# One order of stages for another in the six lists that four engines play, in a two-layer transformer stack

## The reference

```python
x = x + ln(conv(ln(x)))      # filter phazor**t * init, over the 256 positions, through an FFT; y.real
x = x + ln(moe(ln(x)))       # 8 experts (128->64->128), top 2 of a softmax, silu(gate)*up, and a shared expert
x = x + ln(attention(ln(x))) # 16 heads of 64, q and k scaled to unit length, 2 null keys and values,
                             # alibi slopes, causal mask, softmax
x = x + ln(ffn(x))           # top 2 of 4 different experts:
#   e0 = silu(x@w1) * (x@w3) @ w2
#   e1 = gelu(linear chain(x)) @ c2        e3 = gelu(x@ml_w1 + b) @ ml_w2
#   e2: syn = x@w; h = ln(syn + attn(syn)); h = ln(h + relu(h@f1)@f2); h@gen
```

## Time and profile before

| | us |
|---|---|
| median of 3 runs | 1089.22 (1089.21 to 1092.03) |
| profiled execution | 1091.11 |
| its span | 1089.3 |
| PE busy | 967.2 (89%) |
| DVE busy | 815.8 (75%) |
| POOL busy | 585.1 (54%) |
| ACT busy | 568.5 (52%) |
| mean granted clock of TensorE | 0.972 of full speed |

### The profile page before, as it was taken

How to read it: one execution, slowest core, us unless ns; L and a number is a source line. 1 busy time by engine, 2 the same in 40 slices (tenths; PEclk the granted TensorE clock), 3 DMA queues, 4 the chain that set the end, 5 groups by cost and what they waited for, 6 DMA issues and landing times.

```text
span 1089.3 us, 22228 instructions
## 1 busy us (share of the span) xinstructions
PE 967.2 (89%) x8405; PEld 741.4 (68%) x8405; DVE 815.8 (75%) x2425; ACT 568.5 (52%) x1288; POOL 585.1 (54%) x570
## 2 busy tenths in 40 slices
PE   0777899899989999899989999899999999898987
PEld 0566767677766867667777777668776777667755
DVE  5788667978779687887778787886778665793556
ACT  4417642764437552774537643575527653385522
POOL 4227453854557463764737645674627644573623
PEclk9978999999999999999999999999999999899999
DMA  5300000000000000000000000000000000000000
GB/s 154 84 0 10 2 2 2 1 11 2 12 1 1 11 2 11 1 10 2 2 11 1 12 2 11 1 11 2 2 11 1 1 2 2 10 1 2 12 1 11
DMA packets 22091, 11.53 MB, mean 11 GB/s; under 512 B 7648, under 2 KB 21344, under 8 KB 21856
## 3 DMA queue, kind: packets, MB, share of 16 engines
q1 hardware_dynamic: 18272, 8.86, 3.1%
q10 hardware_dynamic: 3712, 1.25, 0.5%
HBM read 8.00 MB, written 2.10 MB: 9 GB/s over the span
## 4 chain that ended last, share of the span: by engine, by line
PE 39%; DVE 34%; POOL 14%; issue 6%; ACT 5%; ACTq 0%; DVEq 0%; POOLq 0%
POOL rnorm L869 9%; PE bank L1909 5%; PE bank L1907 3%; PE bank L1649 3%; PE bank L1870 3%; PE bank L1651 2%; PE bank L1650 2%; PE bank L2042 2%; DVE unit L1483 2%; PE bank L1656 2%; PE bank L2048 2%; DVE sumsq L1474 2%; PE bank L1800 2%; PE bank L1876 2%; DVE x4m L1601 1%
## 5 line engine op out<-in xcount | busy, mean ns | idle before, releaser
L869 POOL TENSOR_TENSOR rnorm<-sumsq,minus_half 128x16 f32<-128x16 f32 x64 | 185.7, 2932 | 11.1 <-DVE sumsq L1477 11.1
L877 POOL TENSOR_TENSOR square<-square,causal 128x256 f32<-128x256 f32 x128 | 97.7, 794 | 87.1 <-ACT square L1111 87.1
L877 POOL TENSOR_TENSOR unit<-unit,causal 128x256 f32<-128x256 f32 x128 | 89.9, 732 | 91.4 <-ACT unit L1111 91.3
L1870 PE MATMUL bank<-qT,kT 64*128 64x256 f32 x512 | 96.6, 389 | 0.0
L1106 ACT ACTIVATE square<-bank,bias_k 128x256 f32<-128x256 f32 x128 | 54.2, 483 | 69.7 <-PE bank L1870 69.6
L1483 DVE TENSOR_TENSOR unit<-unit,rnorm 128x1024 f32<-128x1024 f32 x64 | 79.1, 1240 | 10.5 <-POOL rnorm L869 9.6
L1474 DVE TENSOR_REDUCE sumsq<-square 128x16 f32<-128x1024 f32 x64 | 77.8, 1216 | 9.3 <-ACT square L1066 9.3
L1876 PE MATMUL bank<-qT,kT 64*128 64x128 f32 x512 | 84.1, 284 | 0.7 <-ACT val L1083 0.7
L1059 ACT ACTIVATE unit<-bank 128x512 f32<-128x512 f32 x128 | 72.3, 600 | 23.7 <-PE bank L1651 20.8
L1876 PEld LDWEIGHTS bank<-qT,kT 64*128 64x128 f32 x512 | 71.0, 186 | 16.8 <-issue 10.1
L1045 ACT ACTIVATE xaT_hi<-bank 128x256 fp32r<-128x256 f32 x16 | 6.0, 384 | 144.0 <-PE bank L1808 144.0
(11 more groups left out here) (385 smaller groups left out, 2772.8 us busy)
## 6 DMA issues: line engine op xcount, KB each, us to landing
xin<-in_L_attn_x SPq DMA_DIRECT2D x7, 256.0 KB, 2.8
out<-x SPq DMA_DIRECT2D x7, 256.0 KB, 2.3
square<-in_L_attn_w_kv SPq DMA_DIRECT2D x1, 1024.0 KB, 7.6
w_sw<-in_L_ffn_sw_w SPq DMA_DIRECT2D x3, 256.0 KB, 6.2
unit<-in_L_attn_w_q SPq DMA_DIRECT2D x1, 512.0 KB, 6.7
w_out<-in_L_attn_w_out SPq DMA_DIRECT2D x8, 64.0 KB, 2.1
w_ml<-in_L_ffn_ml_w SPq DMA_DIRECT2D x2, 256.0 KB, 5.7
xin<-in_L_attn_x ACTq DMA_DIRECT2D x1, 256.0 KB, 3.2
```

Of the source, the lines that this page charges most:

```text
L869: pool.tensor_tensor(rnorm[:, k, t, :], sumsq[:, t % 2, k, :], minus_half[:], ALU.pow).then_inc(a_root.sem, 1)
L877: m = pool.tensor_tensor(pd, pd, causal[:].unsqueeze(1).to_broadcast([P, 2, P]), ALU.mult)
L1870: return mm(bank[s][:, 2 * P * i:2 * P * (i + 1)], kT[rs, p, 2 * P * b:2 * P * b + P], qT[rs, p, 2 * P * b:2 * P * (b + 1)], start=True, s ...
```

## The change

All 24 lists (six tables, four engines) hold the same stages as before in another order. No function, no wait and no buffer is changed; all lines behind the tables stand two further down (L1808 before is L1810 after). The first lines of PE's list of the round:

```diff
 MIDDLE = {
     "PE": """
-a_m.0 a_m.1 f_clock f_turn.0 f_turn.1 f_ce.0 f_ce.1 f_sw.0 a_null f_me.0 a_t.0 f_sw.1 f_ceT a_m.2 f_relu.0 a_v.0 f_sw.2
+f_clock a_m.0 a_null f_turn.0 f_turn.1 f_ce.0 f_ce.1 a_m.1 f_sw.0 f_me.0 a_t.0 f_sw.1 f_ceT a_m.2 f_relu.0 f_relu.1
...
-a_out.1 l_x.1
+l_down.3 a_out.0 a_out.1 l_x.0 l_x.1
```

and the part of DVE's list between the routing and the third sum of squares, and its end:

```diff
     "DVE": """
-f_stats.0 f_stats.1 a_ss.0.0 a_ss.0.1 f_apply.1 f_apply.0 a_ss.1.0 a_u.0.0 f_route f_ce a_u.0.1 f_hid.0 f_ce_apply
+f_stats.0 f_stats.1 a_ss.0.0 f_apply.0 f_apply.1 a_ss.0.1 f_route f_ce a_u.0.0 a_u.0.1 f_hid.0 f_ce_apply a_ss.1.0
...
-l_hg.3 l_hu.2 a_mix.3 l_hu.3 e_sum a_mix.4 l_hc.1 l_hg.4 a_mix.5 l_hc.2 l_hc.3 l_hu.4 a_mix.6 f_end a_mix.7 l_dstats.0
-l_end.0 l_dstats.1 l_astats.0 l_aapply.0 l_end.1 l_astats.1 a_o.0 l_aapply.1 l_xl.0 a_end.0 a_o.1 l_xl.1 a_end.1
+e_scan a_mix.2 l_hg.3 l_hc.1 l_hu.3 a_mix.3 a_mix.4 f_end l_hc.2 a_mix.5 e_sum l_hg.4 l_hu.4 l_hc.3 a_mix.6
+l_dstats.0 a_mix.7 l_end.0 l_dstats.1 l_astats.0 l_end.1 l_astats.1 a_o.0 l_aapply.0 l_aapply.1 a_end.0 a_o.1 l_xl.0
+l_xl.1 a_end.1
```

## The result

The changed kernel takes 1054.95 us (median of 4 runs, 1053.46 to 1056.01) against 1090.62 for the kernel before in the same comparison (1089.21 to 1092.56): a ratio of 0.9671, 95% interval 0.9648 to 0.9694, or 35.9 us less. I had said 1068 with a range from 1056 to 1088.

What follows compares the result with a forecast made beforehand. PE was taken as the bound (967.2 of 1089.3 us busy), leaving its waits and low-clock time. Five rounds -10, prologue -1.5, first round -1, last border -4.5, last attention -3.5, last FFN -1: -21.5, giving 1068, range 1056 to 1088.

Steps and rivals of the forecast that it cites:

- the ends: Everything outside the five rounds: prologue, first attention, last border, last attention and last FFN, together 11.5 us off.
- The first attention (FIRST): First round: the same swap of a_out and l_x as in the rounds, without an FFN; -1 us (0 to -1.34).
- Last border: LAST_L to LAST_A: the 3.82 wait shrinks, 2.5 gained, and 2.5 of low clock mostly goes; -4.5 us (0 to -6.3).
- Last attention: Null keys' transpose: the 2.74 wait for null_p and 1.7 of low clock go; -3.5 us (0 to -4.4).
- Prologue: s_null moves to the end of ACT's list, easing PE's 3.17 wait and low clock; -1.5 us (+1 to -4).
- Last FFN: f_ce.1 goes ahead of f_me.0, which waits 0.47; -1 us (+1 to -2).
- The round: Each of five rounds: -1.2 border and FFN transpose, -1.4 later waits, +0.6 POOL; -2.0 a round, -10.0 in all.
- rival 2: The rounds give their full 3.4 us each, 17 + 11.5 = 28.5 off, 1061, low clock also given back; chance 0.16.
- (b): Round border, DVE: the FFN's end, 1.80 us, leaves the row PE waits for and stands in mid-attention, where DVE has time.
- (a): Round border, PE: both halves of a_out play before the transposes, so other matmuls cover the 1.34 us wait.
- the late root: Round, POOL's third root: DVE's sum of squares comes later, POOL stands idle; +0.6 us a round, bounds 0 to 7.0.
- The table load: Round, ACT: load moves among the first tile's copies, costed at nothing; drain rival up to 1.38 a round, 1075, chance 0.05.

Runs made afterwards that it cites:

- t_fhg: Kernel before with one move on DVE in FIRST: l_hg.2 ahead of l_cT and l_hu.1; 1088.90 us.
- t_hg: Kernel before with one stretch of DVE's list in LAST_L reordered: l_hg.1 directly behind a_mix.1, f_end_stats behind l_cT; 1089.06 us.
- t_border: Kernel before with two moves on DVE in LAST_L: f_end ahead of a_mix.6, l_xl.0 ahead of a_end.0; 1091.63 us.
- t_null: Kernel before with two moves in LAST_A: a_nT ahead of a_scores.0 on PE, a_nexp ahead of a_scores.0 on ACT; 1091.09 us.
- t_null3: Kernel before with three moves in LAST_A: a_nT (PE) and a_nexp (ACT) ahead of a_scores.0, a_nexp ahead of f_out.0 on DVE; 1088.47 us.
- t_estats: Kernel before with one swap at the head of DVE's list in PROLOGUE: e_stats ahead of s_phase; 1089.70 us.
- u_fend: Changed kernel with one thing of the round undone: DVE's f_end again between a_mix.6 and a_mix.7; 1050.23 us.
- u_fend_clock: Changed kernel with DVE's f_end again between a_mix.6 and a_mix.7, and PE's clock matmuls again ahead of f_turn; 1047.62 us.

## Why the prediction was wrong in size

What failed is the pricing of the ends: each was given one or two known edits or waits, 11.5 us in all, and they gave 25.1 in the traces. The prediction names 3.82, 2.74 and 3.17 as the larger single waits; the trace before also has 16.99, 8.13 and 3.74 us in the prologue (the last for `ce_rows` at 75.89) and 3.41 in FIRST (for `unit` at 109.92).

- **The first attention (FIRST), the step that failed most.** I priced FIRST by the one edit that I knew from the rounds (a swap at its end, -1) and it gave 7.1. The step never looked at FIRST's own waits. One of them, 1.90 us for L1432 with low clock behind, was worth 2.9 alone (t_fhg). Where the other 4 come from was not taken apart.
- **Last border.** -4.5 was put on the border and nothing on LAST_L's body. Measured: 8.3 for the table, 4.4 of it in the body, where one gate's place is worth 3.5 (t_hg). The border alone gave none that can be told (t_border), and the term "5 us at 0.50, 2.5 back" was wrong: DVE paces that stretch, and with a full clock LAST_A got 0.8 us shorter at most. The rest of the table's 8.3 us needs its other moves; which of them is open.
- **Last attention.** I found 4.4 us in it and took 3.5; 6.0 came. Left out of the sum: 0.86 for `xaT_hi` behind the null keys and 1.24 for a mask late in the mixes, both gone after. That the gain needs DVE's `a_nexp` too I had not seen (t_null, t_null3).
- **Prologue.** -1.5 against 3.8. The term looked at `s_null` on ACT and missed the head of DVE's list: `e_stats` ahead of `s_phase` is 1.7 of it (t_estats). The 3.17 us wait is gone in the trace after; 0.98 at a gate projection (53.04) and 1.25 at an up projection (56.80) stand there, and the clock over 57 to 63 is 0.72, not full.
- **Last FFN.** -1 against 0.3 in the traces; not tried alone.
- **The round.** -2.0 was near: 2.2 in the traces of all tables together, 8.8 us in all with MIDDLE alone. But the parts behind the sum were not what I said. The border's idle time fell by 2.4, not 1.2; the rest of the round, where I had -1.4 + 0.6, lost 1.2: the 1.49 and the 0.74 went, and waits of 1.35 for `unit`, 0.85 for the coefficients and 0.73 for a mask came. The clock behind `x4m`, low in four of five rounds before, is low in all five after, so rival 2 got nothing back there. The move of `f_end` (b), which carried most of my 1.2, costs 0.6 to 0.9 where it was put; the swap (a), priced at 0.6, can't be taken back for less than 3.2; the late root, priced as +0.6 of pure cost, is half of a pair. The sum was right by luck rather than by its terms. What each of the other moves in the round is worth stays open: their effects do not add.
- **The table load.** By the Trainium skill's "ScalarE: Activation LUTs" (section "What ACT_TABLE_LOAD costs") every round would have had some 1.38 us of drain at this load, an estimate from the figure of that page; both traces show 1.28 us and no drain, also with the load in ACT's busy stretch. Here the measurement decides.

I had looked for large single waits. The list of PE's waits by releaser over the whole kernel before (total us, times, the longest) shows the gate chain as one item, larger than any that I priced at the ends; 4.1 of its 8.9 us are the waits of the five rounds, 3.9 the two in FIRST and LAST_L:

```profile
PE bank L1649 <- DVE unit L1432: 8.9, 9, 2.0
...
PE bank L1649 <- DVE xaT_lo L1379: 3.8, 1, 3.8
...
PE bank L1897 <- ACT null_p L1088: 2.7, 1, 2.7
```

## What to carry to other kernels

Where several engines play written lists, price each table of the schedule by its own waits; here the wait at a gate was 0.74 us in a steady round and 1.90 and 2.02 in FIRST and LAST_L. Move a step on all engines that feed it or on none: half of a move cost up to 5.7 us a round here. Read a clock over all rounds and not in one. And before crediting a low-clock stretch, see whether another engine was busy all through it; if so, nothing comes back.

## What was not expected of the hardware

- The same wait in front of the same matmuls is followed by different clocks. In u_fend the wait for `x4m` is 1.31 to 1.34 us in all five rounds; behind four of them the clock is low (0.66 to 0.76 over 5 us), behind the last it is full, and that round is 1.1 to 1.7 us shorter. In u_fend_clock three of four waits of 2.06 us for `xaT_lo` have 0.66 behind them and one 1.00. So a single round or a single trace can't price such a stretch. What decides is open.
- DVE and POOL can lengthen each other's instructions, but not by running side by side as such. The mean root takes 3070 ns after instead of 2932 and the mean multiplication behind it 1341 instead of 1240. In the rounds it comes from one meeting each: a multiplication (L1485) that begins beside POOL's addition L887 takes 2.28 us instead of 1.22, and the root behind it 3.89. The 16 multiplications that lie beside a root for over nine tenths of their time take 1.23 us on average (37 of them before, 1.22). The cause of the meeting's price was not tested.
